# Grouped-query attention on one core: the product and the lower half-plane on GpSimd, the upper half-plane copied by ScalarE, turned planes converted on ScalarE and VectorE

## The reference, cut to what matters

```
q = (x @ wq.T).reshape(b, s, N_HEADS, HEAD_DIM).transpose(0, 2, 1, 3)
k = (x @ wk.T).reshape(b, s, N_KV_HEADS, HEAD_DIM).transpose(0, 2, 1, 3)
v = (x @ wv.T).reshape(b, s, N_KV_HEADS, HEAD_DIM).transpose(0, 2, 1, 3)
qg = q.reshape(b, N_KV_HEADS, groups, s, HEAD_DIM)
scores = jnp.einsum('bhgqd,bhkd->bhgqk', qg, k) * HEAD_DIM ** (-0.5)
attn = jax.nn.softmax(scores, axis=-1)
out = jnp.einsum('bhgqk,bhkd->bhgqd', attn, v)
out = out.reshape(b, N_HEADS, s, HEAD_DIM).transpose(0, 2, 1, 3).reshape(b, s, N_HEADS * HEAD_DIM)
return out @ wo.T
```

## Time and profile before

| | before |
|---|---|
| median of 3 runs | 1860.95 us (1856.93 to 1867.44) |
| the profiled execution | 1863.15 us, span 1861.4 us, mean granted TensorE clock 0.939 |
| TensorE busy | 1627.6 us (87%) |
| VectorE busy | 1118.0 us (60%) |
| ScalarE busy | 864.6 us (46%) |
| GpSimd busy | 751.5 us (40%) |

### The profile page before, as it was taken

One profiled execution on the slowest core, in us unless ns is written; L12 is line 12 of the kernel. 1 busy time (PEld: TensorE's weight loads), 2 busy tenths in 40 slices (PEclk: granted clock), 3 DMA queues, 4 the chain that ended last, 5 costly groups with the idle time before them and its releaser, 6 DMA issues. The chain is left out here.

```text
span 1861.4 us, 25652 instructions
## 1 busy us (share of the span) xinstructions
PE 1627.6 (87%) x8164; PEld 1247.7 (67%) x8164; DVE 1118.0 (60%) x2614; ACT 864.6 (46%) x1620; POOL 751.5 (40%) x882
## 2 busy tenths in 40 slices
PE   5698899987869995889989898998989989979996
PEld 4485555545657874667767776777767767757884
DVE  5561565644384247676766677676677766756235
ACT  2112566651132222665755666566566656731230
POOL 2252555531213631453544545345354444511533
PEclk9797799988889997999999999999999999989999
DMA  2200000001065642444344343433434333453934
GB/s 82 97 1 3 2 4 2 2 2 36 1 253 206 229 139 90 91 102 114 68 105 104 96 106 80 109 88 94 120 90 113 78 91 74 97 178 134 337 119 136
DMA packets 312094, 180.22 MB, mean 97 GB/s; under 512 B 281895, under 2 KB 283767, under 8 KB 309568
## 3 DMA queue, kind: packets, MB, share of 16 engines
q1 hardware_dynamic: 300160, 152.81, 29.1%
q0 software_dynamic: 11840, 26.25, 4.5%
HBM read 111.08 MB, written 22.54 MB: 72 GB/s over the span
## 5 line engine op out<-in xcount | busy, mean ns | idle before, releaser
L1311 POOL TENSOR_TENSOR st_plane<-st_prob,st_rinv 128x512 f16<-128x512 f32 x256 | 312.9, 1223 | 469.9 <-DVE st_rinv L1358 463.1
L1363 DVE SCALAR_TENSOR_TENSOR st_plane<-st_prob,st_rinv,st_plane 128x512 f16<-128x512 f32 x256 | 257.2, 1005 | 62.6 <-POOL st_plane L1311 61.1
L1235 ACT ACTIVATE st_pt<-st_plane_t 128x1024 fp32r<-128x1024 f16 x256 | 269.7, 1055 | 1.0 <-DMA st_plane_t<-st_plane 1.0
L1371 DVE TENSOR_REDUCE st_nmax<-st_score 128x1 f32<-128x512 f32 x256 | 175.1, 686 | 86.8 <-PE st_score L108 83.7
L1250 ACT ACTIVATE st_prob<-st_score,st_nmax 128x512 f32<-128x512 f32 x256 | 175.1, 684 | 40.8 <-DVE st_nmax L1371 40.7
L2004 DVE CUSTOM_DVE_ANT_0 st1b_dump<-st1b_score,st1b_maskrow 128x128 f32<-128x128 f32 (+3 forms) x256 | 112.8, 487 | 89.8 <-PE st1b_score L1702 65.3
L1859 ACT ACTIVATE st1b_slabs<-st1b_across 128x512 f32<-128x512 f32 (+1 forms) x192 | 90.6, 527 | 84.0 <-PE st1b_across L1721 65.5
L614 PE MATMUL st_bank<-st_xts,st_raw 128*128 128x128 f32 x992 | 121.0, 275 | 0.7 <-ACT st_xts L707 0.3
L835 DVE COPY st_ln_xn<-st_bank 128x512 f32<-128x512 f32 x62 | 42.9, 692 | 130.8 <-PE st_bank L621 82.5
L614 PEld LDWEIGHTS st_bank<-st_xts,st_raw 128*128 128x128 f32 x992 | 115.8, 192 | 2.1 <-issue 2.1
L106 PE MATMUL st_outp<-st_pt,st_vhi 128*128 128x512 f32 x256 | 102.3, 399 | 8.7 <-ACT st_pt L1235 8.7
(11 more groups left out here) (377 smaller groups left out, 3924.2 us busy)
## 6 DMA issues: line engine op xcount, KB each, us to landing
st_raw<-in_moe_w SPq DMA_DIRECT2D x40, 768.0 KB, 12.9
sorted_outs<-st_ln_xn SPq DMA_DIRECT2D x62, 256.0 KB
st_qraw<-in_gqa_q SPq DMA_DIRECT2D x8, 1024.0 KB, 5.3
st_oraw<-in_gqa_o SPq DMA_DIRECT2D x8, 1024.0 KB, 5.2
rows<-st_ln_xn SPq DMA_DIRECT2D x2, 2048.0 KB, 9.4
st_kvraw<-in_gqa_kv SPq DMA_DIRECT2D x8, 512.0 KB, 3.8
st_plane_t<-st_plane SPq DMA_TRANSPOSE x256, 2.8
st1a_raw<-in_w_attn SPq DMA_DIRECT2D x3, 1024.0 KB
```

The costliest lines, as they stand in the source:

```text
L1235: act.activation(pt[:, :, t * P:(t + 1) * P], plane_t[t][:, :, :], ACT.Copy).then_inc(pt_ready, 1)
L1311: pool.tensor_tensor(plane[t][:, 0:T], prob[:, t, :], rinv[:, slot:slot + 1].broadcast_to([P, T]), ALU.mult).then_inc(upper_ready, 1)
L1363: dve.scalar_tensor_tensor(out=plane[t][:, T:2 * T], in0=prob[:, t, :], scalar=rinv[:, slot:slot + 1], in1=plane[t][:, 0:T], op0=ALU.mult, ...
L1371: dve.tensor_reduce(nmax[:, slot:slot + 1], score[t][:, :], AX, ALU.max, negate=True).then_inc(nmax_ready, 1)
```

## The change

The work on the probabilities is dealt out anew. GpSimd's first operation on a tile (`scaled`) now writes the product prob * rinv back into prob in float32. ScalarE copies it as float16 into the upper half of the plane (`upper`). GpSimd subtracts that from the product: the lower half (`lower`, moved from VectorE). The turned plane is no longer converted by one instruction of 1024 columns on ScalarE but by two of 512: the upper half on ScalarE (`turned_hi` into `pthi`), the lower half on VectorE (`turned_lo` into `ptlo`). The exponential of a tile now also waits until `lower` of the same tile in the unit before is done, since it overwrites prob.

```diff
-        pt = s.sb("pt", [P, 2 * TB, T], F32R)
+        pthi, ptlo = s.sb("pthi", [P, TB, T], F32R), s.sb("ptlo", [P, TB, T], F32R)
...
                     wait(sp, lower_ready, n + 1)
-                    wait(sp, pt_ready, n - 3)
+                    wait(sp, pthi_ready, n - 3)
+                    wait(sp, ptlo_ready, n - 3)
...
-                    wait(pe, pt_ready, QT * g + 4 * u + 4)
+                    wait(pe, pthi_ready, QT * g + 4 * u + 4)
+                    wait(pe, ptlo_ready, QT * g + 4 * u + 4)
...
+                def turned_hi(g, u, t):
+                    wait(act, turned[t], 16 * (NU * g + u + 1))
+                    act.activation(pthi[:, :, t * P:(t + 1) * P], plane_t[t][:, 0:TB, :], ACT.Copy).then_inc(pthi_ready, 1)
+
+                def upper(g, u, t):
+                    wait(act, norm_ready, QT * g + 4 * u + t + 1)
+                    wait(act, turned[t], 16 * (NU * g + u))
+                    act.activation(plane[t][:, 0:T], prob[:, t, :], ACT.Copy).then_inc(upper_ready, 1)
...
                             wait(act, nmax_ready, QT * g + n + 1)
+                            wait(act, lower_ready, QT * g + n - 3)
                             act.activation(prob[:, t, :], score[t][:, :], ACT.Exp, bias=nmax[:, slot:slot + 1],
                                            accum_out=rsum[:, slot:slot + 1]).then_inc(exp_ready, 1)
+                            if t >= 2:
+                                upper(g, u, t - 2)
                         if u + 1 < NU:
                             q_hi(g, u + 1)
                         elif not final(g):
                             q_hi(g + 1, 0)
+                        upper(g, u, TB - 2)
+                        upper(g, u, TB - 1)
...
+                def scaled(g, u, t):
+                    slot = u % 2 * TB + t
+                    wait(pool, rinv_ready, QT * g + 4 * u + t + 1)
+                    pool.tensor_tensor(prob[:, t, :], prob[:, t, :], rinv[:, slot:slot + 1].broadcast_to([P, T]), ALU.mult).then_inc(norm_ready, 1)
+
+                def lower(g, u, t):
+                    wait(pool, upper_ready, QT * g + 4 * u + t + 1)
+                    pool.tensor_tensor(plane[t][:, T:2 * T], prob[:, t, :], plane[t][:, 0:T], ALU.subtract).then_inc(lower_ready, 1)
...
                         for t in range(TB):
-                            slot = u % 2 * TB + t
-                            wait(pool, rinv_ready, QT * g + 4 * u + t + 1)
-                            wait(pool, turned[t], 16 * (NU * g + u))
-                            pool.tensor_tensor(plane[t][:, 0:T], prob[:, t, :],
-                                               rinv[:, slot:slot + 1].broadcast_to([P, T]), ALU.mult).then_inc(upper_ready, 1)
+                            scaled(g, u, t)
+                            if t >= 1:
+                                lower(g, u, t - 1)
+                        lower(g, u, TB - 1)
...
+                def turned_lo(g, u, t):
+                    wait(dve, turned[t], 16 * (NU * g + u + 1))
+                    dve.tensor_copy(ptlo[:, :, t * P:(t + 1) * P], plane_t[t][:, TB:2 * TB, :]).then_inc(ptlo_ready, 1)
+
...
-                def lower(g, u, t):
-                    slot = u % 2 * TB + t
-                    wait(dve, upper_ready, QT * g + 4 * u + t + 1)
-                    dve.scalar_tensor_tensor(out=plane[t][:, T:2 * T], in0=prob[:, t, :], scalar=rinv[:, slot:slot + 1],
-                                             in1=plane[t][:, 0:T], op0=ALU.mult, op1=ALU.subtract).then_inc(lower_ready, 1)
```

More of the change, by code:

```diff
@@ L1009, in gqa_stage @@
         score_ready, nmax_ready, exp_ready = s.sem("score_ready"), s.sem("nmax_ready"), s.sem("exp_ready")
-        flat_ready, rinv_ready, upper_ready, lower_ready = (s.sem(n) for n in ("flat_ready", "rinv_ready", "upper_ready", "lower_ready"))
+        flat_ready, norm_ready, rinv_ready, upper_ready, lower_ready = (s.sem(n) for n in ("flat_ready", "norm_ready", "rinv_ready", "upper_ready", "lower_ready"))
         turned = [s.sem(f"turned{n}") for n in range(TB)]
-        pt_ready, out_ready = s.sem("pt_ready"), s.sem("out_ready")
+        pthi_ready, ptlo_ready, out_ready = s.sem("pthi_ready"), s.sem("ptlo_ready"), s.sem("out_ready")
         ohi_ready, olo_ready = s.sem("ohi_ready"), s.sem("olo_ready")
@@ L1126, in values @@
                         last = three_passes(pe, outp[u % 2][:, :], col(vhi, b * TB + k), col(vlo, b * TB + k),
-                                            pt[:, k, :], pt[:, TB + k, :], k == 0, k == TB - 1)
+                                            pthi[:, k, :], ptlo[:, k, :], k == 0, k == TB - 1)
                     last.then_inc(out_ready, 1)
@@ L1245, in body @@
                             if u >= 1:
-                                turned_copy(g, u - 1, t)
+                                turned_hi(g, u - 1, t)
                             elif not opening(g):
-                                turned_copy(g - 1, NU - 1, t)
+                                turned_hi(g - 1, NU - 1, t)
                             wait(act, nmax_ready, QT * g + n + 1)
+                            wait(act, lower_ready, QT * g + n - 3)
                             act.activation(prob[:, t, :], score[t][:, :], ACT.Exp, bias=nmax[:, slot:slot + 1],
                                            accum_out=rsum[:, slot:slot + 1]).then_inc(exp_ready, 1)
+                            if t >= 2:
+                                upper(g, u, t - 2)
                         if u + 1 < NU:
@@ L1293, in _ @@
                 for t in range(TB):
-                    turned_copy(LAST, NU - 1, t)
+                    turned_hi(LAST, NU - 1, t)
                 out_hi(LAST, NU - 1)
@@ L1373, in body @@
                                 inverse(g, u, t - 1)
+                            if u >= 1:
+                                turned_lo(g, u - 1, t)
+                            elif not opening(g):
+                                turned_lo(g - 1, NU - 1, t)
                             if t >= 1:
                                 lifted(g, u, t - 1)
-                            if t >= 2:
-                                lower(g, u, t - 2)
                         inverse(g, u, TB - 1)
-                        lower(g, u, TB - 2)
                         lifted(g, u, TB - 1)
@@ L1384, in body @@
                             q_lo(g + 1, 0)
-                        lower(g, u, TB - 1)
                         if has_out(g, u):
@@ L1407, in _ @@
                 add(KV1, 0)
+                for t in range(TB):
+                    turned_lo(LAST, NU - 1, t)
                 out_lo(LAST, NU - 1)
```

2 lines of the change are left out of this document (removed).

## The result

| | before | after |
|---|---|---|
| median of 4 runs each | 1863.9 us (1856.93 to 1867.44) | 1813.83 us (1810.1 to 1817.07) |
| ratio after/before, 95% interval | | 0.9735 (0.9697 to 0.9773) |
| span of the profiled execution, granted clock | 1861.4 us, 0.939 | 1813.5 us, 0.943 |

Predicted were 1845 us and a range of 1815 to 1874. The direction is right, the size is not: the time is that of rival (a), 1813.

The account below looks back on a forecast made before the run. TensorE was taken to bound the kernel, losing 12.6 us a group, 8.8 of it waits. Other units gain 6.5, unit 5 loses 4.1: 2.4 a group, 17 us over groups 0 to 6, so 1845 us, range 1815 to 1874.

Parts of the forecast that it names:

- rival (a): Rival, chance 0.15: unit 5 gets no worse (`lower` 1.04, conversion doesn't lock, unit 4's first maximum not late); 1813 us.
- What bounds the kernel: TensorE bounds, losing 12.6 us a group: 8.8 waits for `add` behind `lower`, 3.0 clock, 0.8 draining and refilling.
- 5.2 + 1.3 + 0.8: All units but 5, before, per group: 5.2 us waits, 1.3 clock, 0.8 refilling; 0.8 left after, gain 6.5.
- A steady unit: Ordinary unit: first product at 3.7 us, `add` done 9.2, last `lower` 14.1; TensorE asks at 11.0, so no wait.
- Unit 5: GpSimd's longer queue delays the first product to 12.8; TensorE waits 7.1 us instead of 3.56; loss 4.1 a group.
- The eight operations of unit 4: GpSimd's four products and four `lower` in unit 4: 10.4 us, ending 15.7 into it.
- The four remainders themselves: GpSimd's remainders of the output weights, ahead of unit 5's first product: 5.50 us, conversions pushing their end to 12.8.
- The start: GpSimd's first product in unit 4, with the late first maximum: starts 5.3 us into the unit.
- The clock: Unit 5, TensorE's slow stretch after its waits: 2.3 us booked instead of 1.7.
- (b): Rival, chance 0.2: ring from maximum to maximum closes, deciding once seven operations each take 0.11 us more; slower, 1876 us.
- (c): Rival, chance 0.2: nothing moves; unit 5 loses 6 us instead of 4.1, gain 3 us in all, 1857 us.
- The sum: Total over groups: 2.4 us in each of groups 0 to 6, 0 in group 7, 17 us gained.

Follow-up runs that it names:

- e1_order: Kernel before, nothing moved between engines; on VectorE the last two `lower` stand behind `add`: 1781.35 us, ratio 0.9555.
- experiment 3: Changed kernel with the turned plane again converted by one 1024-column instruction on ScalarE, none on VectorE: 1817.9 us, ratio 0.9746.
- one dose: Changed kernel with one unused 128 x 64 sum per tile on GpSimd behind the product, 1.3 us a unit: 1831.33 us, ratio 0.9827.
- experiment 4: Changed kernel with all four output weights' remainders moved from GpSimd to VectorE, behind `add` in unit 4: 1815.84 us, ratio 0.9734.
- the last experiment: Changed kernel with ScalarE's last turned conversion ahead of tile 0's upper copy, and two of four output weights' remainders on VectorE: 1809.87 us, ratio 0.9725.

## Why the prediction was right in the mechanism and wrong in the size

**What bounds the kernel, and how `add` comes free.** Right. The other units lost 7.3 us a group before, the prediction's 5.2 + 1.3 + 0.8, and e1_order shows that the order alone did it. The sum is right, two of its parts are not: over groups 1 to 6 the lower clock behind unit 3's wait costs 0.5 us in the mean (unit 4 takes 12.8 and 12.4 in groups 1 and 2, 11.1 in the others) and not 1.3, which I had read in group 2, and refilling costs some 0.3 at each of five waits, 1.6 in all and not 0.8. **A steady unit** came out close: in unit 2 (start 985.96) the first product was 3.6 us in (3.7), `add` done 9.35 in (9.2), the last `lower` done 12.8 in (14.1). The 0.8 us that I left to unit 1 and to refilling didn't stay: 7.3 gained for 6.5.

**Unit 5 is the step that failed.** The forecast had GpSimd's first product of unit 5 at 12.8 us, and a stall of 7.1 us behind it with 2.3 for the clock: a loss of 4.1 us a group against before. Measured is the product at 9.7, a loss of 4.3 us for waits and refilling together and 0.6 for the clock, and so a gain of 0.6. The waits themselves are 2.7 us, below the 4 that I had put down as the sign of rival (a). Of the difference to the forecast, 8.0 against 2.4 a group, this is 4.7 of 5.6. By its terms:

- The eight operations of unit 4: 9.15 us (1016.16 to 1025.31) for 10.4. `lower` has a median of 1.17, in the middle of my bounds, and I had taken the upper one: 0.5 of the 1.25. The rest is that the second product came 0.2 sooner behind the first, that the conversion among them held GpSimd up by 0.2 and not 0.5, and rounding.
- The four remainders themselves: 5.05 (experiment 3) for 5.50. The 5.50 of the earlier trace rows held a delay beside VectorE's `lower`, which the change takes away, and I had added the conversions on top of it.
- The start: 5.1 into unit 4 for 5.3; and unit 4 was a little longer than my 11.0. Together with the above the first product starts at 9.7 and not at 12.8: 1.25 + 0.95 + 0.45 + 0.2 + 0.1 = 2.95 of 3.1, the rest is rounding.
- Behind it all went as written: the last conversion is ready 2.4 us later (2.2), the copy, the query's parts and `add` in their order. All of it comes 2.8 to 2.9 us earlier than predicted, `values` at 12.2 for 15.0, `add` done at 15.1 for 18.0, and since TensorE had been slowed by then, it never waited for `add`.
- The clock: 2.3 us booked; 0 in three groups and 1.27 in three, 0.6 in the mean. The waits come in pieces of 1.34 us or less, not in one of 7.

**A wait that I didn't name.** The output projection of unit 5 reads the remainders of the output weights directly, from 5.7 us in, and GpSimd has the last at 9.8: three waits of 0.38 to 0.49. In my forecast they would have lain inside the longer stall. They break it up; whether that is why the clock held in half of the groups, no run isolated.

**The rivals.** (a) gave the right time, 1813, for partly the right reasons and with luck: it had 6.5 us a group and 4 for group 7, 50 in all; the stage gave 7.9 in each of six groups, 5.6 and 1.5, 55 in all, and stages that the change doesn't touch took 7 of it back in the profiled execution. It asked for a cheap `lower` (1.17 is half of that), a conversion that doesn't lock (true towards GpSimd only) and an early first maximum in unit 4 (2.4 in for 2.9). I gave it 0.15 since "three things have to be so at once", but half of each was enough, since the shortfalls add up over the same queue. (b) began only at about one dose more. (c) was not near. **The sum** over groups left out some things: group 0 gave 5.6 and not 2.4, and in group 7 units 1 to 3 won 1.5 and not 4, unit 5 lost 1.5 and not about 4, and unit 7, which the sum doesn't have, won 1.3.

What stays open: how much of unit 5's loss is due to the four remainders on GpSimd (at most 1.7 us of the product's delay, by the estimate in experiment 4), since both attempts to take them away blocked VectorE instead; what sets the clock's fall in groups 4 to 6 with the same waits; and what the whole change would give with `add` still behind GpSimd's last product, which no run tried.

## What to carry to other kernels

Where the busiest engine waits for a short operation, look at what stands ahead of it in its queue and whom that one waits for, and try the order before moving work: here two moved calls gave 4.5%, and the new division of work 2.7%. The difference sits in unit 5, where GpSimd's queue, with 4.7 us more a unit, is full. A gain in every unit may be paid back in the one unit in which rare work stands in the same queue, so sum the rare unit by itself, with the median and not the upper bound for each of its many terms: a few tenths too much on thirteen operations in a row made 3 us here. Look at the stage by itself as well as at the total, since here stages with the same code moved the total by more than some of the effects. And taking work from that queue helps only if the engine that gets it has nothing urgent behind it.

## What the runs showed of the hardware that I had not expected

- VectorE and GpSimd hold each other up unequally where VectorE has a one-input copy: a conversion of 128 x 512 from float16 took 0.40 us alone and up to 1.32 beside GpSimd, which lost 0.12 to 0.2 us per conversion. For VectorE's subtraction with two inputs from SBUF both lose: with GpSimd's query remainder beside them two took 2.77 where four took 3.98 in all (so, by difference, some 1.2 for the last two, which had hardly any of GpSimd's work beside them), and GpSimd's 1.30 became 1.73.
- GpSimd's subtraction of 128 x 512 took 1.17 us with a float16 input and output, 1.29 in float32 and fp32r; the product with a broadcast column 1.04, whether it writes float16 or float32.
- The same waits in the same unit cost 4.3 us in three groups and 5.6 in three others, for the granted clock alone (1.00 and 0.91 over the unit). In the last experiment the same two waits, 0.6 and 2.2 us, gave 17.06 us at 1.00, 18.7 at 0.91 and 19.7 at 0.83.
